# An attention and MLP block on one core: the prologue by halves in a new order per engine, the first query rope from a second product, the sparse steps spread over the first heads, the fifth score tile in pieces of 384 and 256

## The reference

```python
qc = layernorm(x @ W_cq, q_norm_w, q_norm_b)                    # width 192
q_nope, q_pe = split(qc @ W_q)                                  # per head 128 + 64
k_pe, kv_nope = split(x @ W_ckv)                                # per head 64 + 128
k_nope, v = split(layernorm(kv_nope, kv_norm_w, kv_norm_b) @ W_kv)
q = concat(q_nope, rope(q_pe)); k = concat(k_nope, rope(k_pe))
attn = softmax(causal(q @ k.T / sqrt(192))) @ v
# sparse branch: 8 heads, the 8 tokens with the highest gate each
top = top_k(x @ W_ig, 8);  sel = (x @ W_ip)[top]
sp = softmax(sel @ W_sq @ (sel @ W_sk).T / sqrt(128)) @ (sel @ W_sv)
io = mean over the 8 tokens of (sp @ W_io)[:, :128]             # one column per head
x1 = layernorm(x + (attn + io) @ W_o)
out = layernorm(x1 + (silu(x1 @ wu.T) * (x1 @ wg.T)) @ wd.T)    # wu, wg, wd: ternary weights
```

## Time and profile before

| | us |
|---|---|
| median of 3 runs | 727.49 (726.06 to 728.73) |
| the profiled execution | 727.64 |
| its span in the profile | 725.9 |
| PE busy | 665.2 (92% of the span) |
| DVE, ACT, POOL busy | 469.2, 397.7, 365.8 |

### The profile page before, as it was taken

The page is one execution under the profiler, slowest core; times in us unless marked ns, Lnnn a source line. Parts: engine busy times, 40 slices in busy tenths (PEclk is TensorE's granted clock), DMA queues, the critical chain, the costliest instruction groups (busy, mean ns, idle before and its releaser), DMA issues.

```text
span 725.9 us, 14196 instructions
## 1 busy us (share of the span) xinstructions
PE 665.2 (92%) x4496; PEld 604.1 (83%) x4496; DVE 469.2 (65%) x1293; ACT 397.7 (55%) x940; POOL 365.8 (50%) x313
## 2 busy tenths in 40 slices
PE   5666799999999999999999999999999999898895
PEld 5646689888988898889888888898889888887895
DVE  2675256666766576666666666666656677895895
ACT  3342254756475647565656565656565658544562
POOL 5522254835474447445744575356536644530563
PEclk9866599999999999999999999999999999999998
DMA  6142310371036103710361037103610373000000
GB/s 203 46 130 75 79 51 1 88 154 52 1 89 153 51 0 87 152 51 0 87 152 51 0 87 152 51 0 87 151 51 0 87 217 87 2 1 1 1 31 30
DMA packets 28719, 50.51 MB, mean 70 GB/s; under 512 B 8976, under 2 KB 19472, under 8 KB 28688
## 3 DMA queue, kind: packets, MB, share of 16 engines
q1 hardware_dynamic: 28688, 50.12, 27.5%
HBM read 15.50 MB, written 1.05 MB: 23 GB/s over the span
## 4 chain that ended last, share of the span: by engine, by line
PE 60%; DVE 13%; ACT 12%; issue 10%; POOL 4%; DMA 1%; DVEq 0%; ACTq 0%; POOLq 0%; SPq 0%
PE J L675 10%; PE J L677 9%; PE J L676 9%; PE J L701 4%; DVE PTl L1058 4%; ACT kvraw L1022 3%; PE SC L692 3%; PE SC L690 3%; PE SC L689 3%; PE SC L691 3%; PE SC L688 3%; POOL rstd L607 3%; ACT Pb L959 3%; ACT PTh L941 2%; PE SC L866 2%
## 5 line engine op out<-in xcount | busy, mean ns | idle before, releaser
L1058 DVE TENSOR_TENSOR PTl<-J,PTh 128x512 fp32r<-128x512 f32 (+1 forms) x192 | 102.5, 554 | 75.1 <-ACT PTh L941 74.4
L959 ACT ACTIVATE Pb<-SC,nm 128x128 f32<-128x128 f32 (+7 forms) x128 | 94.8, 740 | 47.0 <-DVE nm L1121 46.2
L1121 DVE CUSTOM_DVE_ANT_0 SC<-SC,mask 128x128 f32<-128x128 f32 (+7 forms) x128 | 97.4, 761 | 28.7 <-PE SC L692 27.1
L941 ACT ACTIVATE PTh<-J 128x512 fp32r<-128x512 f32 (+1 forms) x192 | 88.3, 492 | 10.3 <-PE J L701 9.5
L701 PE MATMUL J<-ident,Pb 128*128 128x128 f32 x576 | 88.0, 280 | 4.7 <-ACT Pb L959 4.5
L675 PE MATMUL J<-PTh,Vh 128*128 128x256 f32 x320 | 88.0, 275 | 4.0 <-DVE PTl L1058 3.8
L676 PE MATMUL J<-PTl,Vh 128*128 128x256 f32 x320 | 89.6, 280 | 0.0
L677 PE MATMUL J<-PTh,Vl 128*128 128x256 f32 x320 | 89.3, 279 | 0.0
L701 PEld LDWEIGHTS J<-ident,Pb 128*128 128x128 f32 x576 | 64.8, 142 | 11.2 <-ACT Pb L959 5.4
L688 PE MATMUL SC<-KNh,QNh 128*128 128x512 f32 (+1 forms) x192 | 69.1, 360 | 0.0
L675 PEld LDWEIGHTS J<-PTh,Vh 128*128 128x128 f32 x320 | 60.2, 188 | 9.0 <-DVE PTl L1058 6.7
(11 more groups left out here) (267 smaller groups left out, 1916.7 us busy)
## 6 DMA issues: line engine op xcount, KB each, us to landing
KD<-RKh SPq DMA_DIRECT2D x32, 256.0 KB, 4.5
KL<-RKl SPq DMA_DIRECT2D x32, 256.0 KB, 5.1
KX<-KX SPq DMA_DIRECT2D x16, 256.0 KB, 2.4
QX<-QX SPq DMA_DIRECT2D x16, 256.0 KB, 2.4
QS<-RQh SPq DMA_DIRECT2D x16, 256.0 KB, 4.0
QS<-RQl SPq DMA_DIRECT2D x16, 256.0 KB, 4.5
r_kv<-in_L_attn_W_ckv SPq DMA_DIRECT2D x8, 384.0 KB, 3.4
r_qn<-in_L_attn_W_qT SPq DMA_DIRECT2D x16, 128.0 KB, 2.7
```

Source lines behind the costliest of these rows:

```text
L941: return act.activation(o, i, ACT.Copy)
L959: act.activation(Pb[i % 2][:, w], SC[i % 2][:, w], ACT.Exp, bias=nm[:, i % 2:i % 2 + 1], scale=-1.0, accum_out=sm[:, b, i:i + 1]).then_inc ...
L1058: dve.tensor_tensor(o, i, h.bitcast(F32), ALU.subtract).then_inc(done[kind], 1)
L1121: dve.tensor_tensor_reduce(out=SC[i % 2][:, w], in0=SC[i % 2][:, w], in1=mask[:, 128 * (7 - i):S], scale=-SCALE, scalar=HIGH, op0=ALU.add, ...
```

## The change

- The host hands over x also transposed (`xT`), W_cq with W_ig in one array, the rope columns of W_q packed per pair (`W_qpe`), the same of pair 0 with the two members of each rope pair swapped (`W_qps`), all norm vectors in one (`vec`), cosine and sine in one. The `xt` transposes go; `xs` takes high and low halves of four quarters of `xT`, of which SP loads two and ACT two.
- PE first issues twelve bf16 products of the mask with itself (`WARM`), whose result is not used.
- The prologue's list is replaced by one per engine (`PRO_PE`, `PRO_ACT`, `PRO_DVE`, `PRO_POOL`), and its steps work on halves of 512 tokens. `qc` writes into the score buffers and is normalised straight from them, in part on ACT (`qnm`), in part on DVE. The swaps, ropes and stack copies of head 0 are done per half, each half with semaphores of its own.
- The query rope of pair 0 needs no swap by DMA: `qps` is a product with the swapped weights, and DVE multiplies both products from PSUM (`rope_q_first`).
- Score tiles 0 to 3 of head 0 need only the first halves. The second halves (`qm` 2 and 3, `qp`, `qps`, `ropeq`, `rk`, `kt`, `qn`, `vsh`) are steps of head 0, and tile 4 waits for them.
- The sparse branch is thirteen steps: 0 to 9 in head 0, 10 to 12 in head 1. `side` 3 and 4 gather one half of the channels each, `side` 5 and 6 take four of the eight heads each. Its buffers move from Pb into QX, and the first `exp` no longer waits for it. `rw` of heads 0 and 1 moves to `LAST`, with two more loads and splits of W_o.
- Tile 4 is written at column 128 of its score buffer, in pieces of 384 and 256, in all heads.

```diff
-        PROLOGUE = (each("xt", 0, 1, 2, 3) + each("wkv", 0) + each("wqp", 0) + each("wqn", 0) + each("wosp", 0) +
-                    each("qc", *range(T)) + each("qrs", 0) + each("kpe", 0, 1) + each("kv", 0, 1) + each("wb", 0) +
-                    each("kv", 2, 3) + each("ropek", 0) + each("qnorm", 0) + each("kvn", 0) +
...
+        PRO_PE = (each("qc", 0, 1, 2, 3) + each("kpe", 0) + each("qc", 4, 5, 6, 7) + each("kv", 0) + each("qm", 0, 1) +
+                  each("kv", 1) + each("ab", 0) + each("qp", 0) + each("qps", 0) + each("kpe", 1) + each("wb", 0) +
+                  each("kv", 2, 3) + each("qm", 2, 3) + each("kt", 0) + each("qn", 0))
...
+            if first and b == 0:
+                return [("qk", 0, 0), ("exp", 0, 0), ("qmb", 0, 2), ("qmb", 0, 3),
+                        ("qk", 0, 1), ("exp", 0, 1), ("qp", 0, 1), ("qps", 0, 1), ("kvn2", 0, 1), *t(0, 0),
+                        ("qk", 0, 2), ("exp", 0, 2), *t(0, 1), ("ropeq", 0, 1), ("rk", 0, 1),
+                        ("qk", 0, 3), ("kt", 0, 1), ("qn", 0, 1), ("exp", 0, 3), ("pv", 0, 0), *t(0, 2), ("vsh", 0, 1),
+                        ("wkv", 1, 0), ("kvn2", 0, 2),
+                        ("qk", 0, 4), ("side", 0, 0), ("side", 0, 1), ("exp", 0, 4), *t(0, 3), ("stk", 1, 0), ("stq", 1, 0),
...
+        def rope_q_first(eng, c):
+            X, q = QX, half(c)
+            eng.wait_ge(ld_cs[c], 16)
+            eng.wait_ge(ready["qp"], c + 1)
+            eng.tensor_tensor(X[:, 0, q], J[bank_of[("qp", 0, c)]][:, :], cosT[:, q], ALU.mult).then_inc(done["qp"], 1)
+            eng.wait_ge(ready["qps"], c + 1)
+            eng.tensor_tensor(X[:, 1, q], J[bank_of[("qps", 0, c)]][:, :], sinT[:, q], ALU.mult).then_inc(done["qps"], 1)
...
+                first = isinstance(pair, int) and pair == 0 and b == 0
+                if first and i % 4 == 0:
+                    c = i // 4
+                    pe.wait_ge(done["qn"], count("qn", h, c))
+                    pe.wait_ge(done["kt"], count("kt", h, c))
+                    pe.wait_ge(k0_stacked[c], 64)
+                    pe.wait_ge(q0_stacked[c], 32)
...
-                for c in range(CHUNKS[i]):
-                    k = slice(512 * c, min(512 * c + 512, 128 * (i + 1)))
+                for k in PIECES[i]:
+                    o = SC[i % 2][:, SHIFT[i]:SHIFT[i] + S - SHIFT[i]]
...
+            pe.wait_ge(const_ready, 1)
+            for n in range(WARM):
+                mm(SC[1][:, 512:1024], lhsT=mask[:, 0:128], rhs=mask[:, 128:640], start=True, stop=True)
...
-                        if isinstance(u, int) and u == 0 and i == 0:
-                            act.wait_ge(done["side"], 11)
```

More of the change, by code:

```diff
@@ L93, in wait, with up @@
             eng.wait_ge(s, v)
+        def up(u):
+            return 0 if isinstance(u, int) and u == 0 else u + 1
         def hold(eng, s, v):
@@ L732, in side @@
-                if c == 4:
-                    pe.wait_ge(ld_wip, 16)
-                    for h in range(IH):
+                    pe.wait_ge(ld_x, 16)
+                    for t in range(T):
+                        last = mm(o[:, 0:64], lhsT=acc[:, t, tile(c - 3)], rhs=oneh[:, t, :], start=t == 0, stop=t == T - 1)
+                    return last
+                pe.wait_ge(w, c - 1 if c == 6 else c)
+                if c in (5, 6):
+                    if c == 5:
+                        pe.wait_ge(ld_wip, 16)
+                    for h in range(4):
+                        q = 4 * (c - 5) + h
@@ L1000, in run @@
                     if kind == "qm":
                         if c == 0:
[L1002 to L1007 removed]
+                            act.wait_ge(ld_vec, 32)
```

657 lines of the change are left out of this document (422 added, 235 removed).

## The result

| | before | changed |
|---|---|---|
| median, us | 727.68 (4 runs, 726.06 to 728.73) | 719.40 (4 runs, 716.64 to 722.12) |
| profiled execution, us | 727.64 | 718.88 |
| its span, us | 725.9 | 717.1 |

The ratio is 0.9897, with a 95% interval of 0.9872 to 0.9921: the changed kernel is about 1% faster, 8.3 us. I had forecast 24 us, and the time lies above my range of 688 to 716.

A forecast was written before the change was run, and what follows sets the result against it. PE was taken to bound the loop, with idle time at the start. Head 2 at 131, plus 725.9 - 154.0 for the rest, minus 2.4 (pieces), plus 1.5 (last pair): 702.0 span, 703.7 us in all; range 688 to 716.

The forecast's parts named there:

- The prologue: Start to first score product: it comes at 34 us (31 to 40) instead of 84.8, a gain of 51 us.
- To the fifth tile: Head 0, first score product to tile 4: waiting for the second halves takes 20 us (16 to 23), PE idling 11.
- From the fifth tile to head 2: Heads 0 and 1: 71 us of work plus 6 of stalls, so head 2 starts at 131 instead of 154.
- the stalls: Between fifth tile and head 2: half clock 2.5, side 2's wait 2.5, other waits 1 or 2; 6 us, bounds 1 to 12.
- The fifth tile's pieces: Fifth tile in the loop: 384 and 256 columns save 0.2 us per head, 2.4 us over 12 heads (0 to 3.1).
- The last pair: Last two heads: the moved sparse rows, splits of W_o, additions and a copy cost 1.5 us (0 to 4).
- The clock: PE idles ahead of the fifth tile and starts it at half clock, costing 2.5 us.
- rival 1: Head 0: second halves are covered, tile 4 comes 10 us after the first score product, not 20; 690 us; chance 0.15.
- rival 3: Head 0: sparse products hold PE's clock at 0.50, adding 30 to 45 us; 740 us, slower; chance 0.02.
- rival 4: Fifth tile: the pieces give nothing because DVE's mask step and the exponential set the pace; 706 us, within the main case.
- rival 2: Prologue: a late DMA or POOL step puts the first score product at 41, fifth tile 23 later; 714 us; chance 0.12.
- the three signs: Wrong if PE's clock stays 0.50 past 65 us, first score product comes after 40, or tile 4's wait is under 5.

The follow-up runs named there:

- e_kpe_io: e_kpe_early with the split of ioT and copy of the output column done after head 1's fifth tile instead of its seventh; 713.9 us (0.9825).
- e_side_early: Changed kernel with side steps 0 and 1 put ahead of head 0's fifth tile on every engine; 718.5 us (0.9876).
- e_no_rw: Changed kernel without the sparse rows of heads 0 and 1 in the last pair, so the output lacks that part; 715.1 us (0.9821).
- e_kpe_early: Changed kernel with pair 1's key products and their POOL rotation moved from head 0's end to right behind side step 6; 716.4 us (0.9845).
- e_best5: e_best4 with the load and split of head 0's rows of W_o moved from slot 2 to slot 6 of head 14; 707.1 us (0.9738).
- e_best4: e_best3 with POOL's split of head 1's weights into Vh and Vl moved behind the splits of the next weights; 706.6 us (0.9724).
- e_best3: e_kpe_io with rope before third tile, query stack first, side steps 0, 1 before fifth tile, step 3 behind pv, sparse rows in head 15; 706.6 us (0.9714).

## Why the prediction was wrong

- **The prologue**: right. Forecast 34, measured 33.3, by the row of steps that I had: the first tiles were normalised at 16.6 (forecast 16.3), DVE's low halves were done at 21.5 (21.2), the rope at 27.0 (27).
- **To the fifth tile**: right. Forecast 20, measured 21.6, with PE idle for 6.1 us ahead of it and for 10.2 in all (11).
- **From the fifth tile to head 2**: this failed. Forecast 77 (71 of work, 6 of stalls, bounds 1 to 12), measured 88.5. The work was right: the sparse products ran at 0.12 to 0.13 each (16 in 1.85 to 2.09 us), and PE was busy for 77.1 us, 12.65 of them at half clock (3.97, 3.40 and 5.28 in its three stretches), which makes 70.8 at full clock, an estimate from these figures. The term that failed is the stalls, 6: PE was idle for 11.4 us, and the half clock added some 6.3, 17.7 together. The term was mis-sized because I went through PE's and DVE's queues there and not through POOL's and SP's. I counted `kpe` of pair 1, which moved from slots 3 and 4 of head 0 to its end, with its products on PE alone, and nothing of what hangs on it: swap, rotation, and the power behind them in POOL's queue. Taken away, that was 3.7 us. The late split of ioT between POOL's operations was 3.0 more in e_kpe_io (1.7 to 3.1 by all kernels that have the move). Of what was left in head 1 (36.3 against 33.8) the 2.25 us of iocol beside POOL and side steps 10 to 12 are candidates; neither was tested. In head 0 stands the 4.0 us wait for i8d, where DVE stood behind POOL; with it gone, head 0 was 1.8 us shorter in e_side_early.
- **The fifth tile's pieces**: the products gained 0.2 in every head, as the sum has it, but the sentence "PE is the bound in the loop, so all counts there" failed in odd heads, where PE then waits for the exponential: 0.17 to 0.26 a pair and not 0.4. That the pair's length came out at 72.75 as forecast, 72.8, was luck: some 0.15 a pair came from elsewhere.
- **The last pair**: forecast +1.5, bounds 0 and 4, measured +3.3 (+3.2 against e_no_rw). The sentence on POOL's first split, "behind it stand only the ternary steps, which wait for later things", was wrong: they wait for DVE's nthr, which is there 17.9 us into head 14, and the split only starts at 18.4. So they came 1.6 us late. How much of the 3.3 us this is stays open.
- **The clock**: behind the first score product it was 0.50 from 35.1 to 41.9, 52.1 to 58.9, 65.8 to 69.2 and, not forecast, 117.0 to 123.8 us; the last three lie in or right behind PE's waits of 6.1, 4.0 and 3.9 us. I had 2.5 us for it, and it was some 6.3 from the fifth tile to head 2. In e_kpe_early the stretch at 117 us went with the wait of 3.9, in e_kpe_io the one at 132.8 us with the wait of 2.4. So a stall can cost more than its own length (2.4 us of wait, 3.0 of gain). But the stretches are not tied to a wait one to one: e_best5 has one at 64.0 to 67.4, e_best4 with the same steps in head 0 has none there.
- **The rivals**: rival 1 (covered) and rival 3 (clock held at 0.50) did not come; rival 4 (the exponential sets the pace around the fifth tile) was right for odd heads; rival 2 came nearest in time, 714, for a wrong reason. None of the three signs by which I would have known myself wrong showed: the clock did not stay at 0.50 past 65 us, the first score product came before 40, the wait ahead of tile 4 was over 5 us. All three watch the prologue and the fifth tile, and the error lay behind them, where "head 2 at 131" was the only mark.

In sum: the 15.1 us of span over the forecast are -0.7 (prologue), +1.6 (fifth tile), +11.5 (from there to head 2), +1.0 (the first pair of the loop, 73.76 us, which I had not told from the others) and +1.8 (last pair), within 0.1.

The best kernels here, e_best3 to e_best5, take 706.6 to 707.1 us, 0.971 to 0.974 of before. They are 3 to 4 us above the predicted 703.7, and only with moves that the change does not have (side steps 0 and 1 ahead of the fifth tile, the rope ahead of the third tile), besides the queues of POOL and SP put in order.
